# Norm rows in fewer transfers, a fifth x buffer, and feature sums on TensorE in the last group of a two-layer attention kernel

## The reference, cut to what matters

```python
def feature_map(x, orf):                       # orf is 128 x 32
    proj = x @ orf.T / d_k ** 0.25
    norm = jnp.sum(x * x, axis=-1, keepdims=True) / (2.0 * math.sqrt(d_k))
    return (jnp.exp(proj - norm) + EPS) / math.sqrt(m)

q = feature_map(split(x @ Wq.T + bq), orf)     # split: 16 heads of 32 columns
k = feature_map(split(x @ Wk.T + bk), orf)
v = split(x @ Wv.T + bv)
kv   = jnp.einsum('nlm,nld->nmd', k, v)
ksum = jnp.sum(k, axis=1)                      # the sum of the key features over the tokens
out  = jnp.einsum('nlm,nmd->nld', q, concat(kv, ksum))
out  = out[..., :-1] / out[..., -1:]
x = layernorm(x + out @ Wo.T + bo)
x = layernorm(x + x @ (ternary(weight) * scale).T)
```

## Time and profile before

| | us |
|---|---|
| median of 3 runs | 1310.12 (1309.89 to 1310.64) |
| the profiled execution, its own time | 1310.11 |
| its span, first to last instruction | 1308.2 |
| PE busy in the span | 1279.2 (98%) |
| DVE busy | 946.1 (72%) |
| ACT busy | 701.9 (54%) |
| POOL busy | 511.1 (39%) |

### The profile page before, as it was taken

How to read it: one execution, slowest core, us unless ns; L and a number is a source line. 1 busy time by engine, 2 the same in 40 slices (tenths; PEclk the granted TensorE clock), 3 DMA queues, 4 the chain that set the end, 5 groups by cost and what they waited for, 6 DMA issues and landing times.

```text
span 1308.2 us, 25147 instructions
## 1 busy us (share of the span) xinstructions
PE 1279.2 (98%) x8570; PEld 965.2 (74%) x8570; DVE 946.1 (72%) x1791; ACT 701.9 (54%) x1403; POOL 511.1 (39%) x1005
## 2 busy tenths in 40 slices
PE   9999999999999999999999999999999999999886
PEld 8767787777877678776787768876788767886655
DVE  7599765886668775787657786577765787657866
ACT  5556535564355743657336663367544665346634
POOL 1325433345333443325424344334453334433343
PEclk9999999999999999999999999999999999999999
DMA  7557314763145721567215762257602675036611
GB/s 237 146 129 217 94 46 111 177 176 91 57 123 145 207 67 55 131 152 193 61 57 129 182 165 67 61 136 200 161 33 70 154 202 140 33 95 140 165 33 65
DMA packets 94015, 160.37 MB, mean 123 GB/s; under 512 B 31168, under 2 KB 47680, under 8 KB 93376
## 3 DMA queue, kind: packets, MB, share of 16 engines
q1 hardware_dynamic: 67856, 139.78, 41.5%
q10 hardware_dynamic: 9648, 16.85, 3.4%
q0 software_dynamic: 16384, 2.13, 1.2%
HBM read 39.13 MB, written 16.78 MB: 43 GB/s over the span
## 4 chain that ended last, share of the span: by engine, by line
PE 83%; DVE 5%; ACT 3%; SPq 3%; DMA 3%; issue 2%; POOL 1%; ACTq 0%; POOLq 0%; DVEq 0%
PE ps L927 27%; PE ps L964 24%; PE ps L1025 8%; PE ps L950 4%; PE ps L996 4%; PE ps L952 4%; PE ps L951 4%; PE ps L983 4%; PE ps L1051 2%; DMA rows<-in_x_t 1%; SPq L519 1%; ACT features L671 1%; SPq L508 1%; DMA rows<-in_Wk_t 1%; DMA stacks<-norm_rows 1%
## 5 line engine op out<-in xcount | busy, mean ns | idle before, releaser
L671 ACT ACTIVATE features<-ps 128x512 f32<-128x512 f32 x512 | 278.3, 601 | 257.3 <-PE ps L927 197.5
L574 POOL DMA_DIRECT2D stacks<-norm_rows x512 | 251.4, 499 | 397.4 <-DVE norm_rows L852 173.7
L553 POOL TENSOR_SCALAR stats<-stats 128x1 f32<-128x1 f32 x128 | 36.4, 284 | 317.9 <-DVE stats L780 317.9
L927 PE MATMUL ps<-Wo_hi,stacks 128*128 128x512 f32 x448 | 150.5, 402 | 0.0
L645 ACT ACTIVATE values_then_attention<-ps 128x512 f32<-128x512 f32 x64 | 38.2, 597 | 197.3 <-PE ps L952 194.0
L793 DVE TENSOR_TENSOR den<-den,features 128x512 f32<-128x512 f32 x192 | 132.3, 689 | 13.8 <-ACT features L671 0.4
L927 PE MATMUL ps<-orf_key_a,stacks 128*128 128x256 f32 x512 | 131.7, 289 | 1.1 <-DMA stacks<-norm_rows 1.1
L1025 PE MATMUL ps<-features,kv_ksum 128*32 128x512 f32 x1024 | 123.1, 598 | 5.9 <-ACT features L671 4.6
L927 PE MATMUL ps<-orf_key_b,stacks 68*128 68x256 f32 x512 | 128.5, 283 | 0.0
L829 DVE SCALAR_TENSOR_TENSOR unit_lo<-ps,cols,unit_hi 128x512 fp32r<-128x512 f32 x128 | 94.3, 736 | 35.0 <-ACT squares L655 35.0
L927 PEld LDWEIGHTS ps<-orf_key_a,stacks 128*128 128x128 f32 x512 | 97.1, 190 | 26.9 <-issue 23.0
(11 more groups left out here) (136 smaller groups left out, 2726.6 us busy)
## 6 DMA issues: line engine op xcount, KB each, us to landing
stacks<-unit_hi SPq DMA_DIRECT2D x384, 128.0 KB, 2.4
stacks<-unit_lo SPq DMA_DIRECT2D x256, 128.0 KB, 3.2
stacks<-unit_hi SPq DMA_DIRECT2D x64, 256.0 KB, 3.8
rows<-in_x_t SPq DMA_DIRECT2D x56, 256.0 KB, 3.6
out<-rows ACTq DMA_DIRECT2D x56, 256.0 KB, 2.0
stacks<-norm_rows POOLq DMA_DIRECT2D x512, 4.0 KB, 2.7
rows<-in_x SPq DMA_DIRECT2D x32, 256.0 KB, 4.0
features<-in_x SPq DMA_DIRECT2D x32, 256.0 KB, 4.1
```

The lines of the kernel that those rows point to most:

```text
L574: pool.dma_start(slot[row:row + 1, c:c + L].rearrange("o (t c) -> o t c", c=DH), NN[DH * h:DH * (h + 1), u % 2, part, :].bitcast(F32)).the ...
L671: nc.scalar.activation(FE[:, n % 8, :, 0:M], ps[:, :].rearrange("p (a m) -> p a m", a=HG), ACT.Exp, scale=C_EXP).then_inc(a_exp.sem, 1)
L927: last = mm(out, a, b, start=(n == 0), stop=(n == len(terms) - 1))
```

## The change

Four edits:

1. `lift_norms` issues 4 transfers for a key unit (two rows from 64 partitions each) and 2 for a query unit (one row of 4096 numbers from 128 partitions) where it issued 8. The bytes and the pieces of 128 bytes are the same. The counts that are waited for follow.
2. x has a fifth buffer, `fifth_x`, for tile 4. Five tiles are loaded in units 2 and 3, three in unit 5, and tiles 5 to 7 take buffers 0 to 2.
3. In the last group of the last batch (`sums_on_pe`) DVE adds no features. Each of the 8 `G` stages gets four more matmuls of 128 columns against ones (float32, so 8 more records), and the four at the end go. ACT no longer waits for DVE's additions there.
4. In the last batch the early `AG` stages are reordered: halves 0 of groups 0 and 1 stand in unit 6 ahead of its last two `F`; `R` of group 2, second half, and half 0 of group 2 open unit 7; the three halves 1 follow in unit 7 where they stood behind `OK` of tile 3. `OK 0 0` stands ahead of `KVT`, `OK 0 1` and `OK 0 2` behind it.

```diff
+def sums_on_pe(b, g):
+    return b + 1 == B and g + 1 == NG
...
+        early = [("AG", b, 0, 0), ("AG", b, 1, 0)] if b + 1 == B and u + 2 == NU else []
...
-            seq = f(0, 1) + p[0] + f(2, 3) + p[1] + s0 + l0 + f(4, 5) + q0 + half + p[2] + f(6, 7) + s1 + l1 + q1 + norm + lift + p[3]
+            seq = f(0, 1) + p[0] + f(2, 3) + p[1] + s0 + l0 + f(4, 5) + q0 + half + p[2] + early + f(6, 7) + s1 + l1 + q1 + norm + lift + p[3]
...
-            seq += [("LX", b + 1, t) for t in range(4)]
+            seq += [("LX", b + 1, t) for t in range(5)]
...
-            seq += [("LX", b + 1, t) for t in range(4, TT) if b + 1 < B] + p[2] + [("GG", b, g, 0), ("R", b, g, 0)] + q0
+            seq += [("LX", b + 1, t) for t in range(5, TT)] + p[2] + [("GG", b, g, 0), ("R", b, g, 0)] + q0
...
-        seq = [("AG", b, k, 0) for k in range(3)] + f(0, 1, 2) + kv + f(3) + [("KVT", b, g)] + f(4, 5) + [("A", b, 0), ("A", b, 1)]
-        seq += [("OK", b, 0, k) for k in range(3)] + [("R", b, g - 1, 1), ("GG", b, g, 0), ("R", b, g, 0, 0), ("AG", b, g, 0, 0)] + f(6, 7)
-        seq += [("OK", b, 1, k) for k in range(3)]
+        seq = [("R", b, g - 1, 1), ("AG", b, 2, 0)] + f(0, 1, 2) + kv + [("AG", b, 0, 1)] + f(3) + [("OK", b, 0, 0)]
+        seq += [("KVT", b, g)] + f(4, 5) + [("AG", b, 1, 1), ("AG", b, 2, 1), ("A", b, 0), ("A", b, 1), ("OK", b, 0, 1), ("OK", b, 0, 2)]
+        seq += [("GG", b, g, 0), ("R", b, g, 0, 0), ("AG", b, g, 0, 0)] + f(6, 7) + [("OK", b, 1, k) for k in range(3)]
...
-    seq = o(3) + [("AG", b, k, 1) for k in range(3)] + [("R", b, g, 1, 0), ("AG", b, g, 1, 0), ("YT", b, 0), ("LN", b, 3), ("Y", b, 1)]
+    seq = o(3) + [("R", b, g, 1, 0), ("AG", b, g, 1, 0), ("YT", b, 0), ("LN", b, 3), ("Y", b, 1)]
...
-        XR = sb("rows", [P, 4, D])
+        XR, X4 = sb("rows", [P, 4, D]), sb("fifth_x", [P, D])
...
-            flat = XR[:, t % 4, :] if b else VA[:, t, :]
+            flat = (X4[:, :] if t == 4 else XR[:, t % 5, :]) if b else VA[:, t, :]
...
-                for h in range(HG):
-                    for part in range(2):
-                        row, c = (2 * DH + 2 * part + h % 2, L * (2 + h // 2)) if is_key(u) else (3 * DH + part, L * h)
-                        pool.dma_start(slot[row:row + 1, c:c + L].rearrange("o (t c) -> o t c", c=DH),
-                                       NN[DH * h:DH * (h + 1), u % 2, part, :].bitcast(F32)).then_inc(n_lifted[u % 2].sem, 16)
+                for part in range(2):
+                    if is_key(u):
+                        for p in range(2):
+                            row, c = 2 * DH + 2 * part, L * (2 + p)
+                            pool.dma_start(slot[row:row + 2, c:c + L].rearrange("o (t c) -> o t c", c=DH),
+                                           NN[2 * DH * p:2 * DH * (p + 1), u % 2, part, :].bitcast(F32))\
+                                .then_inc(n_lifted[0].sem, 16)
+                    else:
+                        row = 3 * DH + part
+                        pool.dma_start(slot[row:row + 1, :].rearrange("o (t c) -> o t c", c=DH),
+                                       NN[:, u % 2, part, :].bitcast(F32)).then_inc(n_lifted[1].sem, 16)
...
-                        act.wait_ge(v_ks.sem, v_ks.nth(b, 7 * (v // 2) + max(r, 1)))
+                        if not sums_on_pe(b, v // 2):
+                            act.wait_ge(v_ks.sem, v_ks.nth(b, 7 * (v // 2) + max(r, 1)))
...
-                elif kind == "F" and is_key(u):
+                elif kind == "F" and is_key(u) and not sums_on_pe(b, u // 2):
...
+                        if sums_on_pe(b, u):
+                            last = mm(kv[rows, 2 * M:3 * M], ones[:, 0:DH], FE[:, r, h, 0:M], start=False, stop=(r == 7),
+                                      tile_position=(0, DH * h), skip_group_check=True)
-                    if r == 7:
+                    if r == 7 and not sums_on_pe(b, u):
```

More of the change, by code:

```diff
@@ L124, in unit_stages @@
             seq.insert(seq.index(("L", 0, 5, 0)) + 1, ("WF", 0, 2))
-            seq += [("WF", 0, 3)] + [("LX", 1, t) for t in range(4)]
+            seq += [("WF", 0, 3)] + [("LX", 1, t) for t in range(5)]
         return seq
     if b + 1 == B:
-        seq = [("AG", b, k, 0) for k in range(3)] + f(0, 1, 2) + kv + f(3) + [("KVT", b, g)] + f(4, 5) + [("A", b, 0), ("A", b, 1)]
-        seq += [("OK", b, 0, k) for k in range(3)] + [("R", b, g - 1, 1), ("GG", b, g, 0), ("R", b, g, 0, 0), ("AG", b, g, 0, 0)] + f(6, 7)
-        seq += [("OK", b, 1, k) for k in range(3)]
+        seq = [("R", b, g - 1, 1), ("AG", b, 2, 0)] + f(0, 1, 2) + kv + [("AG", b, 0, 1)] + f(3) + [("OK", b, 0, 0)]
+        seq += [("KVT", b, g)] + f(4, 5) + [("AG", b, 1, 1), ("AG", b, 2, 1), ("A", b, 0), ("A", b, 1), ("OK", b, 0, 1), ("OK", b, 0, 2)]
+        seq += [("GG", b, g, 0), ("R", b, g, 0, 0), ("AG", b, g, 0, 0)] + f(6, 7) + [("OK", b, 1, k) for k in range(3)]
         seq += [("R", b, g, 0, 1), ("AG", b, g, 0, 1), ("OK", b, 0, 3), ("LN", b, 0), ("OK", b, 1, 3), ("LN", b, 1), ("A", b, 2), ("A", b, 3)]
@@ L344, in attention_kernel @@
         lifted = [Signal("keys_lifted", NG * KEY_LIFTS, 1, 16), Signal("queries_lifted", NG * QUERY_LIFTS, 1, 16)]
-        n_lifted = [Signal("norms_lifted_even", 2 * HG * NG, 0, 16), Signal("norms_lifted_odd", 2 * HG * NG, 0, 16)]
+        KEY_NORMS, QUERY_NORMS = 4, 2
+        n_lifted = [Signal("norms_lifted_even", NG * KEY_NORMS, 0, 16), Signal("norms_lifted_odd", NG * QUERY_NORMS, 0, 16)]
         def unit_lifted(eng, b, u):
@@ L355, in norms_lifted @@
             if b or u >= 0:
-                eng.wait_ge(sig.sem, sig.nth(b, 2 * HG * (u // 2 + 1)))
+                eng.wait_ge(sig.sem, sig.nth(b, (KEY_NORMS if is_key(u) else QUERY_NORMS) * (u // 2 + 1)))
         s_ld, s_k, s_act, s_pool = (sem(n) for n in ("setup_loaded", "setup_consts", "setup_w_hi", "setup_ones"))
@@ L472, in _ @@
                             wait(s_tern, KT)
+                    elif t == 4:
+                        if b > 1:
+                            wait(*x_split(b - 1, 4))
                     else:
-                        wait(*x_split(b, t - 4))
+                        wait(*x_split(b, t - 5))
                     load_x(b, t)
@@ L480, in _ @@
                     elif b + 1 < B:
-                        wait(*x_split(b + 1, t + 4))
+                        wait(*x_split(b + 1, t + 5 if t < 3 else t))
                     else:
@@ L590, in _ @@
                     elif b + 1 == B and t < 4:
-                        pool.wait_ge(v_glo.sem, v_glo.nth(0, 5))
+                        pool.wait_ge(v_glo.sem, v_glo.nth(0, groups.index((NG - 1, 0, 1)) + 1))
                     if b == 0 and t == 0:
```

## The result

The changed kernel takes 1302.78 us (median of 4 runs, 1302.42 to 1303.04), the kernel before 1310.38 beside it on the same chip: ratio 0.9943, 95% interval 0.9929 to 0.9958. That is 7.6 us less, against a forecast of 8.7 (1301.4). Its profiled execution took 1302.63, with a span of 1300.8; the one of before took 1310.11, so 7.5 of the 7.6 us can be followed from trace to trace.

A forecast was written before the change was run, and what follows sets the result against it. PE was taken as the bound, busy 1279 of 1308 us, so only its idle time or work counts. 2.8 (fifth buffer) + 1.1 (norms) + 4.8 (last batch) = 8.7 us off 1310.11 gives 1301.4; range 1299.5 to 1307.

The forecast's parts named there:

- The fifth buffer: Unit 5 of seven batches: x loads no longer late, PE's 4.6 us wait for exponentials shrinks by 2.8 us.
- Norm rows: Third batch: fewer norm transfers end PE's wait for norms, 1.1 us off; in other units nothing changes.
- The issue: POOL's time to issue one larger query norm transfer: taken as 0.50 to 0.6 us, bounds 0.50 and 2.
- The stall of unit 7 and the clock: Last batch: PE's 2.4 us norm stall goes, and the 1.8 us lost to the slow clock behind it.
- Sums on PE: Last group: 64 records added, 8 removed, heads fully overlapping at 0.22 us per eight; 1.5 us more on PE.
- Rivals 1 and 4: 1 has its own line; 4: last group's `G` and sums without overlap plus a start gap, 1311.7 to 1317; chance 0.05.
- rival 1: Heads' sums overlap partly: two at a time 1304.8; far end, strict order, 1.28 us per token tile, 1308.2; chance 0.20.
- The last batch: Chain of waits from unit 7 on: PE's second turn comes 4.8 us earlier, and so does the end.
- two more ahead of `R`, which cost 0.1: Last batch, DVE: two further low parts ahead of `R` reduce the lead from 3.2 to 3.1 us.
- The waits for normed rows: Last batch: about 5 of PE's 6.3 us of waits stay, being latency of DVE, POOL and ACT.
- Rival 2: Norm issue grows with pieces, or POOL stops in the last query unit; proportional issues give 1305.9; chance 0.08.
- rival 3: The extra x load or the load of tile 5 takes back the 2.8 us: 1304.2; chance 0.07.

## Why the prediction was right, and what was wrong in it

- **The fifth buffer (2.8).** The wait in unit 5 went from 4.6 to 2.1 us, so 2.5 in the trace. The size is right beside the kernel before. That tile 5 would find its load landed is wrong: ACT now waits for it, in the third batch 0.49 us, and 8.4 us for x tiles in all (14 times) where it was 7.5 (12 times). These waits stand behind the exponentials that PE needs, so they cost PE nothing.
```profile
435.24 1.36 ACT L655 ACTIVATE x_hi<-rows 128x512 fp32r<-128x512 f32 x2 [0.49 <-DMA rows<-in_x_t]
```
  As a price of the edit in the changed kernel 2.8 is wrong: there it carries 12 to 13 us (1.0041 without it, 0.9943 and 0.9949 with it), because the other edit makes the loads it hides slower.
- **Norm rows (1.1).** The wait in the third batch went, the stops of POOL too. The step priced the edit on POOL alone and asked only whether an issue costs more; it did not ask what the new form of the transfer does to the DMA engines and so to the loads beside it. With four buffers that costs 0.56% (0.9985 to 1.0041, 7.3 us). The traces make it 11.2 us more in unit 5 and 3.8 less for norm rows. With five buffers the same edit gains some 5 us instead. The two terms came out right as a sum (3.9, against 4.1 by the marks, of which the two waits explain 3.6), and neither can be had alone. That the sum holds is luck in part: the slower loads were not foreseen, and a buffer that was priced for another reason hid them.
- **The issue (0.50 to 0.60).** 0.59 for the query's; 0.68 for the key's, outside what was taken. It changed nothing, since 2.7 us are still under 3.9.
- **The stall of unit 7 and the clock (2.4 and 1.8).** Both gone, as forecast: no wait for norms, clock at 1.00. What was not foreseen is how far the clock counts in the other runs: the kernel before, and the changed kernel with eight transfers again, ran in most of their executions at a lower mean clock than in their fastest ones, and the changed kernel did not. Part of the gain in the medians may be that; how much stays open.
- **Sums on PE (1.5 more).** Right: 0.22 us for eight records. Rivals 1 and 4 are out. The far end of rival 1 was miscounted, without consequence: by the count that gives eight records five places of 0.107 us, sixteen take 13 places, 1.39 us, not 12 and 1.28. Putting the sums back on DVE costs 0.4 to 1.2 us by the ratios and 1.1 to 1.6 to PE's last turn in the traces.
- **The last batch (4.8).** Mis-sized: 3.3. `KVT` came 2.1 us earlier by the marks (2.6 forecast), `GG` 2.8 (3.2), DVE's transpose of `R` only 1.9 where 3.1 was forecast, PE's second turn 4.0 (4.8), its third 3.5, and the end 3.3. The step that failed is "two more ahead of `R`, which cost 0.1": it took the low parts at 0.69 each, and they took 2.53 together, 1.2 more, since POOL's additions, which the same semaphore releases as before, now run beside them. That cost 0.9 on the way to `R`. A second such meeting at 1259.56 cost DVE 1.0, and PE's third turn 0.5 of it: "from that turn on nothing is changed" failed there. In the trace of before the same meeting can be read (DVE's subtraction at over three times its 0.42, and POOL's additions beside it), and it wasn't:
```profile
1274.63 2.52 POOL L594 TENSOR_TENSOR features<-features,out_bias 128x512 f32<-128x512 f32 x2
1274.67 1.42 DVE L890 TENSOR_TENSOR x_lo<-values_then_attention,x_hi 128x256 fp32r<-128x256 f32 x1 [0.48 <-ACT x_hi L700]
```
- **The waits for normed rows.** About 5 us were to stay of 6.3; 5.3 stayed.

Rival 2 (issue or stop) and rival 3 (the load takes the gain back) did not come, though the four-buffer run shows that later x loads, which rival 3 feared, did happen, from another cause.

## What to carry to other kernels

Fewer transfers are not the same work in bigger pieces: look at the outermost dimension of the new form, and at the landing times of the loads beside it, before pricing the edit by its issues. When a subtraction or addition with both operands in SBUF is moved on DVE, look at what POOL runs at the new place as well as at DVE's own gap. Two edits that each look worth 1 to 3 us can hang on each other by 10; take each back once, in the presence and in the absence of the other.

## What the runs showed of the hardware

- A DVE subtraction from SBUF beside a POOL addition: 1.44 us instead of 0.43 (128x256), two of 128x512 2.53 instead of 1.29. DVE's transpose from PSUM beside such additions kept its 0.72 (1245.12 us of the kernel with rows 0 and 1 after the low parts, where POOL added from 1245.04 on).
- fp32 matmuls on four column tiles run side by side though each head has four neighbouring records: 0.22 us for eight of 128 columns. They do not start in the order of the program: all eight records of `G` ahead of the first of the sums.
- POOL's stop between two issues: 1.7 us every 80 transfers with eight per unit (2.0 the first time), 1.44 every 60 with eight and two, none in 192 with four and two. What the list counts, and why the last form never fills it, stays open.
- Key transfers of two rows: 2 packets of 4096 B (293 ns) and 14 of 128 B (150 ns) each, and x loads of 256 KB land in a median of 4.3 to 4.6 us in every kernel that has them, against 3.5 to 3.7 in every kernel without.
- The clock fell to 1.2 GHz for 3.41 us behind an idle of PE of 2.4 us (kernel before), 1.7 (sums on DVE), 2.2 (eight transfers, four buffers) and 2.3 (few transfers, four buffers, at 920 us). It didn't behind the 1.8 and the 2.2 of the kernel with eight transfers and five buffers. The longest wait for ACT near the end, 2.07 us at the line of `YT` in thirteen traces, was followed by a fall in eight traces (3.41 us, and 6.83 in the one with the old order) and by none in five, the changed kernel's and the one of before among them. Every trace ends at 1.2 GHz; that last fall is not counted here. So the idle alone doesn't decide it, and two traces of one kernel can differ by such a fall.
